# One order for two streams of score matmuls: exponentials and maxima in turns instead of block by block

## The reference

```python
scores = jnp.einsum('bhid,bhjd->bhij', q, k) / scale
scores = scores + _alibi_bias(N_HEADS, seq_len, M_SLOPE, x.dtype)[None]   # -|i-j| * slope of the head
attn = jax.nn.softmax(scores, axis=-1)
out = jnp.einsum('bhij,bhjd->bhid', attn, v)
```

## Time and profile before

| | |
|---|---|
| median of 3 runs | 640.96 us |
| the profiled execution's own time | 641.92 us |
| its span | 640.1 us |
| PE busy | 532.1 us (83%) |
| DVE busy | 397.9 us (62%) |
| ACT busy | 344.2 us (54%) |
| granted TensorE clock, mean over the span | 0.908 |

### The profile page before, as it was taken

One profiled execution on the slowest core, in us unless ns is written; L12 is line 12 of the kernel. 1 busy time (PEld: TensorE's weight loads), 2 busy tenths in 40 slices (PEclk: granted clock), 3 DMA queues, 4 the chain that ended last, 5 costly groups with the idle time before them and its releaser, 6 DMA issues.

```text
span 640.1 us, 11471 instructions
## 1 busy us (share of the span) xinstructions
PE 532.1 (83%) x4355; PEld 287.2 (45%) x4355; DVE 397.9 (62%) x654; ACT 344.2 (54%) x669; POOL 215.8 (34%) x394
## 2 busy tenths in 40 slices
PE   6679999999999999999999989998923306999920
PEld 4324444444454545445454444453422304888720
DVE  3688777787987586997767798864063321222217
ACT  4137666676677676766867666775612111223314
POOL 5544643101134051046114115500406140355440
PEclk9688999999999999999999999997965556999985
DMA  7622242223222222222211222100101002334124
GB/s 155 168 80 77 68 140 82 78 90 112 81 86 91 73 94 81 76 68 65 64 39 47 56 85 75 49 11 4 33 16 33 0 15 66 113 108 130 49 94 122
DMA packets 46999, 47.61 MB, mean 74 GB/s; under 512 B 12941, under 2 KB 36671, under 8 KB 46946
## 3 DMA queue, kind: packets, MB, share of 16 engines
q1 hardware_dynamic: 38610, 31.68, 17.6%
q0 software_dynamic: 5488, 12.73, 6.4%
q10 hardware_dynamic: 2848, 2.49, 1.2%
HBM read 31.42 MB, written 16.06 MB: 74 GB/s over the span
## 4 chain that ended last, share of the span: by engine, by line
PE 69%; DVE 16%; DMA 7%; ACT 3%; issue 3%; POOL 2%; ACTq 0%; SPq 0%; POOLq 0%; DVEq 0%
PE ps L772 31%; PE ps L810 16%; DVE row_max L1203 7%; PE ps L941 6%; PE ps L953 5%; PE ps L775 4%; PE ps L836 1%; DMA max_dram<-max_turned 1%; DVE heads L1255 1%; DMA k_stacks<-k_dram 1%; DMA k_dram<-parts 1%; DVE x_tok L1408 1%; PE ps L854 1%; PE ps L824 1%; PE ps L930 1%
## 5 line engine op out<-in xcount | busy, mean ns | idle before, releaser
L1203 DVE TENSOR_REDUCE row_max<-ps 128x1 f32<-128x1024 f32 x256 | 297.0, 1212 | 88.7 <-PE ps L772 46.2
L1056 ACT ACTIVATE probs<-ps 128x512 f32<-128x512 f32 x512 | 268.0, 606 | 89.0 <-PE ps L775 49.7
L772 PE MATMUL ps<-k_stacks,q_stacks 96*128 96x512 bf16 x512 | 165.3, 390 | 14.5 <-DVE row_max L1203 5.2
L772 PE MATMUL ps<-q_stacks,k_stacks 99*128 99x512 bf16 x512 | 164.8, 385 | 4.1 <-ACT probs L1056 2.7
L810 PE MATMUL ps<-probs,v_unit 128*32 128x256 f32 x2048 | 125.3, 386 | 0.0
L775 PE MATMUL ps<-distance,slope_eye 128*128 128x128 bf16 x512 | 113.9, 222 | 0.0
L772 PEld LDWEIGHTS ps<-k_stacks,q_stacks 96*128 96x128 bf16 x512 | 44.0, 99 | 95.4 <-DVE row_max L1203 35.0
L810 PEld LDWEIGHTS ps<-probs,v_unit 128*32 128x32 f32 x2048 | 60.5, 110 | 54.5 <-issue 11.2
L772 PEld LDWEIGHTS ps<-q_stacks,k_stacks 99*128 99x128 bf16 x512 | 49.0, 98 | 57.7 <-ACT probs L1056 20.8
L775 PEld LDWEIGHTS ps<-distance,slope_eye 128*128 128x128 bf16 x512 | 50.7, 99 | 26.0 <-issue 2.4
L1124 ACT ACTIVATE probs<-ps 128x640 f32<-128x640 f32 x32 | 22.5, 705 | 67.9 <-PE ps L941 67.9
(11 more groups left out here) (183 smaller groups left out, 412.5 us busy)
## 6 DMA issues: line engine op xcount, KB each, us to landing
k_stacks<-k_dram SPq DMA_DIRECT2D x62, 144.0 KB
q_stacks<-q_dram SPq DMA_DIRECT2D x62, 72.0 KB
k_stacks<-in_c_alibi_k SPq DMA_DIRECT2D x32, 96.0 KB
w<-in_w SPq DMA_DIRECT2D x12, 256.0 KB, 2.9
xd<-blank POOLq DMA_DIRECT2D x8, 325.0 KB, 2.8
probs<-xd SPq DMA_DIRECT2D x8, 325.0 KB, 3.7
out_dram<-out_t SPq DMA_DIRECT2D x16, 128.0 KB
yt<-zeros POOLq DMA_DIRECT2D x4, 512.0 KB, 3.0
```

The source lines that it names most:

```text
L772: mm = pe.matmul(out, lhs, rhs, start=True, stop=not on_diagonal)
L1056: act.activation(probs[:, k % KEPT, HALF * e:HALF * (e + 1)], ps[:, n % RING, :], ACT.Exp).then_inc(ring_read, 1)
L1203: dve.tensor_reduce(row_max[:, m % 2, i:i + 1], max_pair(k).rearrange("p a n -> p (a n)"), AX.X, ALU.max).then_inc(mx_used, 1)
```

## The change

Within a block, the two exponential products and the two max halves are issued in turns: E0, M0, E1, M1, where it was M0, M1, E0, E1. The waits stay with their instructions. Only PE's program changes; the instructions of the other engines and their order are the same.

```diff
@@ -909,11 +909,10 @@
                             pe.wait_ge(max_loaded[m % SLOTS], 16 * turn_of(m))
                             if m + 2 < UNITS:
                                 pe.wait_ge(loaded[(m + 2) % SLOTS], 16 * loads_by(m + 2))
-                        if m + 2 < UNITS:
-                            for h in range(2):
-                                max_half(m + 2, j, h)
                         for e in range(2):
                             exp_half(m, j, e)
+                            if m + 2 < UNITS:
+                                max_half(m + 2, j, e)
                     if group == 1:
                         values(m, 0)
                     elif m > 0:
```

## The result

The changed kernel took 653.47 us (median of 6 runs, 651.61 to 656.75) against 640.77 us for the kernel before (6 runs): ratio 1.0209, with a 95% interval of 1.0176 to 1.0243. Forecast were 653.0 us and a slowdown. The profiled execution of the changed kernel took 651.61 us, the fastest of its six; its span is 649.8 us, 9.7 above before. So the profile accounts for 9.7 us, and the median for 12.7.

The account below looks back on a forecast made before the run. PE bounds the stretch with maxima, and its groups would now wait for DVE's reduces. 11.4 (single groups) + 0.5 (late groups) - 0.2 (unit 0) + 0.3 (behind the last) = 12.0 us, median 653.0, range 645 to 658.

Parts of the forecast that it names:

- R + 2.41: Earliest start of a group's fourth M0: R, the start of DVE's first reduce behind the group's start, plus 2.41 us.
- Diagonal groups: In the stretch with maxima, 25 such groups reach their values at 4.52 us instead of 4.27: 0.25 slower each.
- Plain groups: In the stretch with maxima, 26 such groups reach their values at 4.34 us instead of 4.14: 0.20 slower each.
- The groups that DVE enters late: Seven groups where DVE's backlog sets the first reduce: +0.07 us each, +0.5 in all, bounds -2 and +1.7.
- Behind the last group: After the last group with maxima, DVE's chain of the second attention starts 0.55 us later, 0.25 already counted: +0.3 us.
- the -0.2 of unit 0: Unit 0's second group follows its first without values between, so only the shorter end shows: -0.2 us.
- The first: Rival, chance 0.11: diagonal groups absorb the delay and only plain groups pay, 647 us.
- second: Rival, chance 0.05: ACT, fed 0.5 us earlier at a group's head, gains what DVE loses: 631 us.
- fourth: Rival, chance 0.06: order within a block doesn't matter, since values give DVE time to catch up: 641 us.
- The third: Rival, chance 0.03: some 100 new pauses drop PE's clock to half for a tenth of the groups: 31 us, 684.

Follow-up runs that it names:

- e3: Order E0, E1, M0, M1 (both exponential products first, max pair together) against the kernel before; 644.32 us against 642.84, ratio 1.0023.
- e7: The kernel before with DVE's reduce over one bank of the pair (512 columns) instead of both; 628.1 us against 643.39 for before, ratio 0.9765.
- e8: The changed kernel with DVE's reduce over 512 columns, one bank of the pair; 629.11 us against 643.39 for the kernel before, ratio 0.9781.
- e4: The changed kernel measured once more, on the chip of three other orders; 656.16 us against 642.84 for the kernel before, ratio 1.0198.
- e1: Order E0, M0, M1, E1 (one exponential product ahead, max pair together) against the kernel before; 643.84 us against 642.84, ratio 1.0016.
- e12: 1, 3, 1, 3 exponential products ahead of a group's four whole max pairs, ACT's output copy later, against the kernel before; 641.41 us against 640.18, ratio 1.0011.
- e5: Turns (E0, M0, E1, M1) in the diagonal groups alone, against the kernel before; 648.91 us against 643.39, ratio 1.0076.
- e10: 1, 1, 3, 3 exponential products ahead of a group's four whole max pairs, against the kernel before; 653.5 us against 643.83, ratio 1.0151.
- e9: Values split, half behind a group's second block and half behind its fourth, ACT's output copy moved, against the kernel before; 650.32 us against 643.83.
- e6: Turns (E0, M0, E1, M1) in the plain groups alone, against the kernel before; 648.31 us against 643.39, ratio 1.0072.

## Why the prediction was right

**What bounds the stretch.** Right: R + 2.41 for the fourth M0. It gave 3.11 before; after, 3.66 and 3.54 were worked out and 3.66 and 3.55 measured. It also held in e3, for an order that the prediction hadn't treated.

The waits are where they were forecast, at M0 of the third and of the fourth block: in the plain group above these start at 2.42 and 3.55, in the diagonal one at 2.53 and 3.66. e7 and e8 confirm the cause: with a short reduce the two orders take the same.

**The size per group.** Diagonal groups: 0.25 worked out, 0.25 measured (25 groups, 6.2 us). Plain groups: 0.20 worked out, 0.225 measured (26 groups, 5.85 us in place of 5.2). The missing 0.02 to 0.03 lies for the most part between the last M0 and the values, which I had as 0.80: it is 215.50 - 214.68 = 0.82. R is 0.01 later too.

**The groups that DVE enters late.** +0.5 in all was taken, +0.33 measured: between -0.07 and +0.14 each. The group of the earlier trace rows went from 5.55 to 5.49. Here R is DVE's own:

```profile
280.50 0.39 PE L772 MATMUL ps<-q_stacks,k_stacks 99*128 99x512 bf16 x1
...
282.78 3.42 DVE L1202 TENSOR_REDUCE row_max<-ps 128x1 f32<-128x1024 f32 x3
...
286.00 1.93 PE L810 MATMUL ps<-probs,v_unit 128*32 128x256 f32 x32
```

The first reduce starts 2.28 us behind the group's start, 0.22 later than before, and the shorter end gives 0.28 back.

**Behind the last group.** The chain of the earlier trace rows costs 0.3 more, as predicted: from the values at 432.46 to the next, whose row starts at 440.06, it was 7.60 us; now it is 7.90:

```profile
448.00 0.31 ACT L1074 ACTIVATE sc_e<-sc 128x128 f32<-128x128 f32 x1 [4.13 <-DVE sc L1282]
...
451.34 1.08 PE L810 MATMUL ps<-probs,v_unit 128*32 128x256 f32 x8
```

**What it had not seen.** One term that adds to the loss and a larger one that takes from it. PE's late matmul L873 waits for DVE twice, and DVE is now later, 0.38 us in all. One of the two, after:

```profile
274.17 0.19 PE L873 MATMUL ps<-hot_any,before 128*128 128x32 bf16 x1 [0.77 <-DVE hot_any L1327]
```

And at 96 us PE waited before for a DMA:

```profile
96.31 0.39 PE L772 MATMUL ps<-k_stacks,q_stacks 96*128 96x512 bf16 x1 [1.20 <-DMA q_stacks<-max_dram]
```

With the change PE gets there only at 95.89 and doesn't wait; that gives back 1.26. In e4, the same kernel, 0.36 of wait remained there. The sum of the stretch is then 6.2 + 5.85 + 0.33 + 0.38 - 1.26 = 11.5, which is the 11.54 measured. Forecast for the stretch were 11.4 + 0.5 = 11.9: the -0.2 of unit 0 lies ahead of it and the 0.3 behind. That it comes so near is in part luck: without the wait for the DMA, of which the forecast knew nothing, the stretch would have lost 12.8.

**The median.** 12.0 above before was forecast, 12.7 measured, 9.7 in the profile. The stretch is settled (387.3 in this profile, 387.7 in e4's), and with the 0.3 behind it it makes 11.8 or 12.2. What makes the rest, the profiles show in part. The profile of e4, the same kernel, has a span of 655.1 us where the one above has 649.8; 2.8 of these 5.3 lie between the end of the stretch and the last values, and there the granted clock differs. Busy times and clock of that part, for before, after and e4:

```profile
432.46:460.10 27.64, 23.54 (x190) 9.22 (x188) 8.69 (x25) 17.42 (x37) 7.53 (x13) 0.88 0.08 20
443.44:470.50 27.06, 22.36 (x190) 8.83 (x189) 8.99 (x26) 16.93 (x36) 7.53 (x13) 0.94 0.08 21
443.93:473.75 29.82, 25.34 (x190) 9.86 (x188) 8.99 (x26) 16.93 (x36) 8.61 (x13) 0.83 0.07 19
```

The same 190 matmuls take longest where the clock is 0.83. The order doesn't fix it: the same kernel has 0.94 and 0.83 in two executions, e1 has 0.94 and 27.4 us there, e12 0.83 and 29.7. In the six runs of the changed kernel, too, the time goes with the clock granted over the whole span, from 651.61 us at 0.917 to 656.75 at 0.909. So the forecast, which had nothing for this, is right to within what such runs differ by, and that the median lies only 0.5 us from it is partly luck. Why the later stages get the one clock or the other stays open, as do 2.0 us behind the last values in e4.

**The rivals.** The first, second and fourth fell. Diagonal groups don't absorb the delay: they pay 0.25 each, in the change and in e5. Feeding ACT earlier gains nothing: the weight loads' waits for ACT went from 9.8 us to 2.3 (the earlier trace rows has them before), and neither diagonal nor plain groups got shorter in the change or in e1 to e3, so these were not stalls of PE. The order within a block matters, by 2.1%. The third fell by the clock of 1.00 (the places where PE's weight loads wait for DVE are 44 more, not the 100 more pauses that the prediction had).

## What to carry to other kernels

A producer that fills a double buffer in several pieces holds the buffer from the first piece to the last. In a short burst with a consumer slower than the producer, the burst ends at (start of the consumer's train) + (its steps) + (what stands behind the last buffer's first piece), so pieces of one buffer belong together, and other work goes between buffers: splitting them cost 1.9 to 2.1% here. Where in the cycle the whole buffer stands hardly mattered (0 to 0.4%) until a second consumer with its own ring was starved (1.5% in e10), so work out both before moving more. A wait for a DMA that PE just meets hides part of such a loss or adds to it.

## What the runs showed of the hardware

- Reduces of 1.21 us followed one another 1.13 us apart, and exponentials shown with 0.6 us 0.49 apart where ACT had work waiting. Lengths of rows would have given 2.49 in place of 2.41 for the fourth M0.
- A switch between the bf16 stream and the small f32 matmuls and back cost 0.2 us (e9), though the engine is shown as busy through it.
- PE waited at 96 us for the load of the maxima in several kernels. It went on at 96.31 before, at 96.45 in e1 and at 96.33 in e9, after waits of 1.20, 1.50 and 2.40 us (at 95.00 in e6 and 94.12 in e12, whose stretch begins 2 us earlier). Behind the first two the clock stayed up. Behind the third PE issued its matmuls 0.43 us apart and took 3.70 us for two blocks in place of 2.20; the row for the 3 us shows a granted clock of 0.50, the lower of the two levels (1.2 GHz):

```profile
97.00:100.00 3.00, 3.00 (x12) 1.18 (x9) 2.15 (x2) 1.52 (x3) 0.00 (x0) 0.50 0.27 98
```

- It was so behind the last group with maxima too: PE stood still for 2.42 us before the change, and from 440 to 444 us the granted clock was 0.50 (the values that start at 440.06 took 3.64 us in place of 1.93).
- Delays of a max half by 0.1 to 0.3 us, two in each of 51 groups, left the granted clock at 1.00, and so did single pauses of 1.0 to 1.5 us.
